# Two attention hops of a graph network on one core: a wait split in halves, another order of steps on four engines, and idle matrix products in another place

## The reference, cut to what matters

```python
def agg(x):
    a_input = jnp.concatenate([x[head], x[tail]], axis=-1)
    e = jnp.sum((a_input @ fc_w.T + fc_b) * rel_e, axis=-1)
    e = jnp.where(e > 0, e, 0.2 * e)
    m = jax.ops.segment_max(e, head, num_segments=N)
    ex = jnp.exp(e - jax.lax.stop_gradient(m)[head])
    denom = jax.ops.segment_sum(ex, head, num_segments=N)
    w = ex / denom[head]
    agg_emb = jax.ops.segment_sum(x[tail] * w[:, None], head, num_segments=N)
    return agg_emb + x
...
for _ in range(n_hops):
    x = agg(x)
    norm = jnp.maximum(jnp.linalg.norm(x, axis=-1, keepdims=True), 1e-12)
    x = x / norm
```

## Time and profile before

| | |
|---|---|
| median of 3 runs | 6296.62 us (6289.2 to 6297.54) |
| the profiled execution, its own time | 6300.04 us |
| its span in the profile | 6298.3 us |
| busy, share of the span: TensorE products, VectorE, ScalarE, GpSimd | 86%, 74%, 69%, 56% |
| first hop, steady octets | 3616 to 4221 us |
| second hop, steady octets | 4352 to 5137 us |
| start of the last layer, to which the page's chain goes back | about 5252 us |

### The profile page before, as it was taken

The page is one execution under the profiler, slowest core; times in us unless marked ns, Lnnn a source line. Parts: engine busy times, 40 slices in busy tenths (PEclk is TensorE's granted clock), DMA queues, the critical chain, the costliest instruction groups (busy, mean ns, idle before and its releaser), DMA issues. The chain is left out here.

```text
span 6298.3 us, 140674 instructions
## 1 busy us (share of the span) xinstructions
PE 5399.7 (86%) x29822; PEld 4623.0 (73%) x29927; DVE 4687.1 (74%) x16868; ACT 4372.7 (69%) x15048; POOL 3545.3 (56%) x3366
## 2 busy tenths in 40 slices
PE   6536999996699998999999888886777777999999
PEld 2326999985588786789999777765666666888887
DVE  9995999996655553267777666665777776989898
ACT  1965999992244442268888688885888875777777
POOL 0776777767666666744444566655445544444443
PEclk9668999998899999999999888886777778999999
DMA  1045777778766666667777688886777874444443
GB/s 51 3 9 155 213 212 211 212 202 253 221 189 198 192 196 196 193 206 222 222 222 222 188 262 266 264 246 182 245 240 241 246 210 124 126 126 127 127 126 119
DMA packets 1164303, 1175.22 MB, mean 187 GB/s; under 512 B 307119, under 2 KB 1038422, under 8 KB 1163283
## 3 DMA queue, kind: packets, MB, share of 16 engines
q1 hardware_dynamic: 1012692, 956.04, 50.3%
q0 software_dynamic: 151360, 216.47, 13.5%
HBM read 963.01 MB, written 393.59 MB: 215 GB/s over the span
## 5 line engine op out<-in xcount | busy, mean ns | idle before, releaser
L218 POOL DMA_INDIRECT landing_first<-messages,by_dst_meta x768 | 824.7, 1074 | 664.5 <-PE l1b_ps_b L1581 369.2
L218 POOL DMA_INDIRECT landing_last<-x,by_dst_meta x384 | 432.8, 1127 | 568.3 <-PE l_ps_a L1718 484.9
L2039 POOL DMA_INDIRECT landing_last<-z,by_src_meta x408 | 433.9, 1063 | 453.8 <-PE l2b_ps_g L2305 318.6
L2039 POOL DMA_INDIRECT landing_last<-x,by_src_meta x408 | 415.9, 1019 | 262.9 <-PE l2a_ps_g L2305 135.5
L218 POOL DMA_INDIRECT landing_first<-in_x,by_src_meta x384 | 399.9, 1041 | 189.3 <-PE l_ps_a L1013 119.0
L1535 ACT ACTIVATE l1a_x_t<-l1a_ps_x,by_dst_first 128x256 f32<-128x256 f32 x400 | 167.9, 471 | 394.6 <-PE l1a_ps_x L1567 391.7
L1579 PE MATMUL l1b_ps_b<-root,l1b_x_t 128*128 128x256 f32 x1600 | 425.9, 389 | 0.0
L1579 PE MATMUL l1a_ps_b<-root,l1a_x_t 128*128 128x256 f32 x1584 | 417.5, 386 | 2.5 <-issue 1.2
L1023 PE MATMUL l_ps_b<-l_w,l_both 128*128 128x256 f32 x1624 | 418.2, 380 | 0.0
L1026 PE MATMUL l_ps_b<-l_w,l_agg_t 128*128 128x256 f32 x1624 | 417.1, 379 | 0.0
L1737 PE MATMUL l_ps_b<-l_w,l_mix_t 128*128 128x256 f32 x1592 | 396.5, 392 | 8.7 <-DVE l_mix_t L1654 7.0
(11 more groups left out here) (417 smaller groups left out, 17921.1 us busy)
## 6 DMA issues: line engine op xcount, KB each, us to landing
l_both<-in_x_both SPq DMA_DIRECT2D x416, 256.0 KB, 4.0
z<-l2a_result SPq DMA_DIRECT2D x400, 152.0 KB, 4.5
x<-l1b_result SPq DMA_DIRECT2D x392, 152.0 KB, 3.0
l2a_x<-x SPq DMA_DIRECT2D x48, 1216.0 KB
l1b_x<-h SPq DMA_DIRECT2D x408, 128.0 KB
l1b_res<-x SPq DMA_DIRECT2D x408, 128.0 KB
l1a_x<-x SPq DMA_DIRECT2D x404, 128.0 KB, 2.9
l_x<-x SPq DMA_DIRECT2D x402, 128.0 KB, 2.3
```

Source lines behind the costliest of these rows:

```text
L218: pool.indirect_dma_start(gathered[:, slot, 0:D], None, source[0:count, :], bass.IndirectOffsetOnAxis(ap=rows, axis=0), bounds_check=limit ...
L2039: pool.indirect_dma_start(gathered[:, k, :], None, x_in[0:N_NODES, :], bass.IndirectOffsetOnAxis(ap=rows, axis=0), bounds_check=limit, oob ...
```

## The change

- Splits the wait in `add_self`: the first part waits for the first rows that it writes over (3), the second for all eight.
- Splits `find_nodes` in three steps (`find_nodes`, `find_masks`, `find_kinds`) that stand at different places of VectorE's order. The wait for `e_done` stays with the mask alone, and SyncE waits for mask and names' matrix both before it loads new names.
- Splits `spread` in two halves; in the second hop one goes ahead of the last part of the aggregation.
- Second hop, TensorE: the look-up goes ahead of both turns, and 14 idle products stand between look-up and turns, where 4 stood behind the turns.
- Second hop, VectorE scales four rows and ScalarE four, where it was three and five; other orders on VectorE and ScalarE.
- First hop, ScalarE: `guess` moves from the front of the order to between the two halves of the exponentials.

```diff
@@ -1779,7 +1779,7 @@
             .then_inc(self.done, 1)
 
 
-SCALED_BY_DVE = 3
+SCALED_BY_DVE = 4
 
 
 class Octet:
@@ -1937,6 +1937,8 @@
                     if octet.after(2):
                         sp.wait_ge(s["masked"], octet.number - 1)
                         sp.sem_inc(s["passed"], 1)
+                        sp.wait_ge(s["hot"], octet.number - 1)
+                        sp.sem_inc(s["passed"], 1)
                     sp.dma_start(row[:, octet.both, :], node_rows[bass.ds(octet.item, OCT), :].partition_broadcast(P))\
                         .then_inc(in_row[octet.half], 16)
 
@@ -2085,11 +2087,17 @@
                     pass_wait(dve, s, in_row[o.half], (o.lap + 1) * 16)
                     if o.after(2):
                         pass_wait(dve, s, s["looked"], o.number - 1)
-                        pass_wait(dve, s, s["e_done"], o.number - 1)
                     dve.tensor_scalar(hot_t[:, o.both, :], row[:, o.both, :], c.item_id[:, 0:1], None, ALU.is_equal)\
                         .then_inc(s["hot"], 1)
+
+                def find_masks(o):
+                    pass_wait(dve, s, in_row[o.half], (o.lap + 1) * 16)
+                    if o.after(2):
+                        pass_wait(dve, s, s["e_done"], o.number - 1)
                     dve.tensor_scalar(mask[:, o.both, :], row[:, o.both, :], c.item_id[:, 0:1], MASK, ALU.not_equal, ALU.mult)\
                         .then_inc(s["masked"], 1)
+
+                def find_kinds(o):
                     dve.tensor_tensor(kind[:, o.both, :],
                                       graph.meta[:, bass.ds(o.item, OCT), KIND].unsqueeze(2).broadcast_to([P, OCT, R2]),
                                       c.iota[:, 0:R2].unsqueeze(1).broadcast_to([P, OCT, R2]), ALU.is_equal)\
@@ -2124,8 +2132,8 @@
                     if h == 0:
                         pass_wait(dve, s, s["guarded"], o.number + 1)
                         pass_wait(dve, s, *o.landed(in_x))
-                        if not last_hop and o.after(1):
-                            pass_wait(dve, s, s["out_ready"], o.item - (OCT - 1))
+                    if not last_hop and o.after(2):
+                        pass_wait(dve, s, s["out_ready"], o.item + (end + 1 - HOP))
                     for j, k in o.each()[first:end]:
                         q = k % OCT
                         dve.wait_ge(s["agg_done"], o.item + bank_end(q))
@@ -2215,16 +2223,15 @@
                 dve.sem_inc(s["out_ready"], 1)
                 square, weigh, improve = (lambda o: inv.square(dve, o)), (lambda o: inv.weigh(dve, o)), (lambda o: inv.improve(dve, o))
                 if last_hop:
-                    steps = [(add_residual, 0), (guard, 1), (centre, 0), (scores, 2),
-                             (part(add_self, 0), 1), (part(add_up, 0), 1), (part(add_self, 1), 1), (part(add_up, 1), 1),
-                             (have_variance, 0), (find_nodes, 3), (maximum, 2), (have_square, 1),
-                             (lambda o: inv2.square(dve, o), 0), (lambda o: inv2.weigh(dve, o), 0),
-                             (lambda o: inv2.improve(dve, o), 0), (square, 1), (shift_bias, 0), (weigh, 1), (improve, 1),
-                             (scale_some, 0)]
+                    steps = [(add_residual, 0), (find_kinds, 3), (centre, 0), (scores, 2), (guard, 1), (part(add_self, 0), 1),
+                             (part(add_up, 0), 1), (find_nodes, 3), (find_masks, 3), (have_variance, 0), (part(add_self, 1), 1),
+                             (part(add_up, 1), 1), (maximum, 2), (have_square, 1), (lambda o: inv2.square(dve, o), 0),
+                             (lambda o: inv2.weigh(dve, o), 0), (lambda o: inv2.improve(dve, o), 0), (square, 1),
+                             (shift_bias, 0), (weigh, 1), (improve, 1), (scale_some, 0)]
                 else:
-                    steps = [(guard, 1), (find_nodes, 3), (scores, 2), (have_square, 0),
-                             (part(add_self, 0), 1), (part(add_up, 0), 1), (maximum, 2),
-                             (part(add_self, 1), 1), (part(add_up, 1), 1), (square, 0), (weigh, 0), (improve, 0)]
+                    steps = [(guard, 1), (find_nodes, 3), (scores, 2), (have_square, 0), (find_kinds, 3), (part(add_self, 0), 1),
+                             (part(add_up, 0), 1), (maximum, 2), (part(add_self, 1), 1), (part(add_up, 1), 1), (square, 0),
+                             (find_masks, 3), (weigh, 0), (improve, 0)]
                 run_octets(dve, graph, steps)
 
             @block.scalar
@@ -2280,9 +2287,9 @@
                     steps = [(lambda o: norm.square(act, o, result), 0), (lambda o: measure(o, 0, 4), 1),
                              (lambda o: measure(o, 4, 4), 1), (lambda o: inv2.guess(act, w.shift, o), 0),
                              (lambda o: inv.guess(act, w.shift, o), 1), (part(chances, 0), 2), (part(chances, 1), 2), (decay, 2),
-                             (apply, 0), (part(take_chances, 0), 2), (part(take_chances, 1), 2)]
+                             (part(take_chances, 0), 2), (apply, 0), (part(take_chances, 1), 2)]
                 else:
-                    steps = [(lambda o: inv.guess(act, w.shift, o), 0), (lambda o: measure(o, 0, 3), 1), (part(chances, 0), 2),
+                    steps = [(lambda o: measure(o, 0, 3), 1), (part(chances, 0), 2), (lambda o: inv.guess(act, w.shift, o), 0),
                              (part(chances, 1), 2), (decay, 2), (part(take_chances, 0), 2), (lambda o: measure(o, 3, 5), 1),
                              (part(take_chances, 1), 2), (part(scale_rows, 0), 0), (part(scale_rows, 1), 0)]
                 run_octets(act, graph, steps)
@@ -2305,18 +2312,19 @@
                             last = pe.matmul(out, hot[:, q, :], gathered[:, o.landing * OCT + q, cols], start=True, stop=True)
                         last.then_inc(s["agg_done"], 1)
 
-                def spread(o):
-                    o.wait(pe, s["score"])
-                    o.wait(pe, s["masked"])
-                    for h in range(2):
-                        first = o.base + h * 4
-                        if o.after(1):
-                            pe.wait_ge(s["made"], o.number * 2 + (h - 1))
-                        pe.matmul(ps_e[:, h * 4:h * 4 + 4, :], c.ident_b[:], mask[:, first:first + 4, :], start=True, stop=False)
-                        for q in range(4):
-                            last = pe.matmul(ps_e[:, h * 4 + q, :], score[:, first + q:first + q + 1].broadcast_to([P, P]),
-                                             c.ident[:], start=False, stop=(q == 3))
-                    last.then_inc(s["e_done"], 1)
+                def spread(o, h):
+                    if h == 0:
+                        o.wait(pe, s["score"])
+                        o.wait(pe, s["masked"])
+                    first = o.base + h * 4
+                    if o.after(1):
+                        pe.wait_ge(s["made"], o.number * 2 + (h - 1))
+                    pe.matmul(ps_e[:, h * 4:h * 4 + 4, :], c.ident_b[:], mask[:, first:first + 4, :], start=True, stop=False)
+                    for q in range(4):
+                        last = pe.matmul(ps_e[:, h * 4 + q, :], score[:, first + q:first + q + 1].broadcast_to([P, P]),
+                                         c.ident[:], start=False, stop=(q == 3))
+                    if h == 1:
+                        last.then_inc(s["e_done"], 1)
 
                 def turn_chances(o, h):
                     pe.wait_ge(s["chance"], o.item + h * 4 + 4)
@@ -2340,12 +2348,13 @@
                     keep_busy(pe, c, ps_spare, n)
 
                 if last_hop:
-                    steps = [(part(aggregate, 0), 1), (part(aggregate, 1), 1), (part(aggregate, 2), 1), (part(aggregate, 3), 1),
-                             (spread, 2), (part(turn_chances, 0), 2), (look_up, 3), (part(turn_chances, 1), 2),
-                             (part(fill, 4), 2)]
+                    steps = [(part(aggregate, 0), 1), (part(aggregate, 1), 1), (part(aggregate, 2), 1), (part(spread, 0), 2),
+                             (part(aggregate, 3), 1), (part(spread, 1), 2), (look_up, 3), (part(fill, 14), 2),
+                             (part(turn_chances, 0), 2), (part(turn_chances, 1), 2)]
                 else:
-                    steps = [(part(aggregate, 0), 1), (part(aggregate, 1), 1), (spread, 2), (part(aggregate, 2), 1),
-                             (part(aggregate, 3), 1), (part(turn_chances, 0), 2), (look_up, 3), (part(turn_chances, 1), 2)]
+                    steps = [(part(aggregate, 0), 1), (part(aggregate, 1), 1), (part(spread, 0), 2), (part(spread, 1), 2),
+                             (part(aggregate, 2), 1), (part(aggregate, 3), 1), (part(turn_chances, 0), 2), (look_up, 3),
+                             (part(turn_chances, 1), 2)]
                 run_octets(pe, graph, steps)
 
 
```

## The result

The changed kernel takes 6061.92 us (median of 4 runs, 6050.15 to 6065.91), the kernel before, run beside it, 6296.93 us (4 runs). The ratio is 0.9626, 95% interval 0.961 to 0.9643: faster by 235 us. The prediction had the direction and both places right, but said 6150 and at best 6100.

A forecast was written before the change was run, and what follows sets the result against it. No engine was full; waits in the ring of handoffs ScalarE, TensorE, VectorE, ScalarE bound both hops. First hop 48 plus second 100 gave 148 us off 6300.04, less 3.4 to the median: 6150 us, range 6100 to 6260.

The forecast's parts named there:

- (2): First hop, ScalarE: the guess, moved between the halves of the exponentials, delays four exponentials by 0.5 us.
- (3): First hop, VectorE: mask (0.5 us) and kinds (0.35) move behind the maximum or into idle time and cost nothing.
- The ring: Second hop, one second guess to the next: VectorE's 6.05 us plus ScalarE's 8.55, sum 14.6 us an octet.
- (4): Second hop, TensorE: look-up and 14 idle products ahead of both turns; ScalarE's 59.8 us wait goes, 1.3 us an octet.
- (5): Second hop: ScalarE's first copy precedes its scalings, so TensorE aggregates during them; half the spread precedes the last aggregation.
- (7): Second hop, VectorE: the maximum goes behind the sums' second half, which fill VectorE while TensorE ends the spread.
- (6): Second hop: VectorE scales a fourth row, 0.35 us more there, 0.52 less on ScalarE.
- (8): Second hop, SyncE: early look-up lets the residual load earlier; VectorE's 41.4 us wait goes, 0.9 us an octet.
- A: First hop gains nothing, as the guess gives back 0.5 us and TensorE keeps standing; 6197 us, chance 0.15.
- B: Both hops: transfers become the bound if DMA engines sustain no more than about 0.85; 6225 us, chance 0.12.
- C: Second hop: idle products hold up the turns at low clock, octet about 18.2 us; 6345 us, chance 0.09.
- D: Both hops: the changes cancel and the hops keep their lengths; 6297 us, chance 0.06.

The follow-up runs named there:

- the whole wait: Changed kernel with the first hop's sums again waiting for all eight scaled rows: 6151.68 us, ratio 0.9759; on the slower chip 0.9831.
- the halved residual: Changed kernel loading only 128 of the residual's 256 columns in the second hop, that part of the sum left out: 6064.98 us, 0.9634.

## Why it was wrong in size

The sum was 48 + 100 = 148. The steady parts gave 78 + 146 = 224, and the ends, which the prediction left unchanged, 15. The direction and the two waits that had to go were right. Two terms of the sum were mis-sized, and the range's lower end with them.

**First hop, the term "I take 12.1".** Measured 11.46, so 78 for 48. Two things in it were off. "ScalarE's own 11.1" was taken as a floor. It is the time in which any instruction of ScalarE was under way, and it isn't a pace: an instruction starts before the one ahead of it has ended (the exponentials last 0.36 us and start 0.344 apart), so each idle piece adds the end of the instruction before it. The same instructions are busy for 495.32/46 = 10.77 us an octet after the change, with fewer idle pieces among them; single ones are shorter too (exponentials 377 to 362 ns, squares 440 to 423), for a reason that no run shows. From start to start, as the timeline after gives them, a full octet is 8 x 0.344 (exponentials) + 0.46 (copy) + 5 x 0.40 (squares) + 0.47 (copy) + 3.52 (scalings) + 3 x 0.40 (squares) + 0.45 (guess) = 10.85 us. The short octets take 10.87: nothing was left of "0.5 to 0.6 for a remainder". And "in the long octet the split alone gives only that 0.3" fell: with the split alone long octets lost 1.58 us (14.12 to 12.54), short ones 1.52. The spread that was late came late from TensorE's standing ahead of the turn, which lay on the same ring; that piece is 1.10 us now in every one of the 46 octets.

**"Octets come in two kinds."** That was read from two octets. By the maxima, 19 of the 46 octets before took 12.38 to 12.39 us, ten 12.55 to 13.02, thirteen 14.12 to 14.55, three 15.21 to 15.29, and one 10.82. The 3.11 us of standing, too, were those of the octet shown: TensorE stood that long in three of the 46 octets and 2.66 to 2.67 us in 19.

**"If TensorE no longer stands 3 us, the long octets go."** It doesn't, and 16 of 46 are still long. Before, the clock fell in each of the 22 octets in which TensorE stood 2.66 us or more, and in one more in which it stood 1.80. That agrees with the rule of the Trainium skill that the prediction cites (TensorE: Matmul & The Clock Gate, HAM oscillation — how this bites in real kernels), by which a wait that repeats in every round takes the clock down each time. After the change it doesn't tell the kinds apart any longer: the wait of 1.10 us ahead of the turn repeats in every octet, it is the only standing piece of over 0.25 us in all octets but one short one, and the clock falls in every second or third octet alone. What makes it fall there stays open. What it costs is known: 16 x 1.67 = 27 us, an estimate of what the hop would gain if all octets were short.

**(2) The guess, 0.5 us.** No cost in the change, which is as quick in this hop as the split alone. **(3)** nothing, as said. With the whole wait (2) and (3) together show in the short octets, 12.82 for 12.39 us.

**Second hop, the term "I take 14.9".** Measured 13.90, so 146 for 100. The ring, worked out as 14.6, is 13.74 in the timeline of the octet shown. VectorE's half, from the second guess's end to the next norm square, was 6.05 and is 5.65; ScalarE's was 8.55 and is 8.09, as the 0.4 of waiting for the maximum isn't there and both guesses take 0.86, not 1.0. The rest, 0.3 to 14.9, was put on because VectorE and the DMA engines come within an eighth of full. Neither asks it: VectorE runs 93% busy, the DMA engines at 0.96, and ScalarE at 98% sets the pace. The prediction's lower bound of 13.7, ScalarE's own, was the answer, and one scaling more shows it (14.17 for 13.74 in the typical octet).

**The range's lower end.** "Both hops at their lower bounds" took 1.4 and 2.9 us an octet, that is 11.75 and 14.17. The second is not the bound of 13.7 that the prediction had worked out itself (3.37 us, 155 in all); with it the end would have been 6300 - 64 - 155 - 3 = 6078. That still leaves out the measured 6061.92. With the 10.87 of the short octets in the first hop too, which no hop of 46 octets reached, it would have been 6300 - 105 - 155 - 3 = 6037.

**(4)** Right for TensorE's order: with the old one 155 us shrink to nothing, and the look-up's place alone gives 56 in the kernel before. Ten of the fourteen idle products are worth nothing to the time; the last four were taken out on the slower chip alone, where the octet did not grow either. **(5), (7)** Either ScalarE's order or VectorE's can be taken out of the change without loss (13.90 and 13.85 us). In the kernel before with the look-up moved, ScalarE's order takes the octet from 16.22 to 14.18 us. What stands in for it in the run without it (VectorE's order, the spread's half ahead, the fourth row) no run takes apart. **(6)** 7 to 14 us. **(8)** The residual's 41.4 us went to 6.6, and the cause is as said: with the look-up alone moved the wait is gone, and in the change with TensorE's old order it is 30.5 us.

**The rivals.** A fell by the split alone. B fell by the share of 0.96 and by the halved residual. C's idle products were to cost 1.1 us an octet. Between look-up and turns fourteen give the same octet as four within 0.1 us; in their place of rival C, in the kernel before, they cost nothing clear of noise on the slower chip, and the other chips did not run them there. D fell by the result.

**Open.** Why the clock falls in 16 octets of the first hop; what makes octets of 15 to 22 us on the slower chip; and whether a scaling moved to VectorE shortens the first hop, which the one run of it could not show. No kernel ran that is faster than the change beyond its interval; the one with 4 idle products is its equal (0.962 to 0.9626).

## What to carry to other kernels

When a ring of handoffs loses its waits, it falls back to the pace of its fullest engine where nothing else holds it (16 octets of the first hop stayed 1.67 us above that pace, those in which the clock fell): take that pace from start to start of its instructions, not from the busy sum plus a margin, and put the range's end there. Sum the gain of waits on one ring together: an octet's late spread was the echo of the wait that was split. Before an order is changed on four engines, change one: here two moved steps gave 133 of the 146 us in the second hop's steady octets, and ten idle products raised the clock and bought nothing, because TensorE was not what others waited for.

## What the runs showed of the hardware

The 16 DMA engines worked at a share of 0.94 to 0.97 over 500 us and more, 295 to 300 GB/s, without being the bound. The kernel before took 6294 to 6302 us on three chips and 6789 to 6791 on another, 8% more; there the change's first hop moved 230 GB/s at a share of 0.75 (0.94 and 298 GB/s on the first chip), and the same edit, the split, was worth 15 us instead of 78.
